# Differential attention with an expert gate: the copy of the gathered output rows is made by VectorE instead of ScalarE

## The reference, cut to what matters

```python
q, k, v = (einsum('bsd,od->bso', xn, w) for w in (wq, wk, wv))   # xn = layernorm(x), x is 4 x 1024 x 256
# 8 heads; q and k of each head are two maps (m = 0, 1) of 32 columns, v is 32 columns
attn = softmax(q @ k.T / sqrt(32) + causal, axis=-1)              # per head and map, 1024 x 1024
attn = attn[:, :nh] - attn[:, nh:] * lmbda                        # map 0 minus lambda times map 1
out = attn @ v                                                    # then an RMS norm in groups, and wo
x = x + (out_normed @ wo.T) * silu(ffn(xn))                       # ffn: 8 experts, 2 chosen for a row
```

## Time and profile before

| | |
|---|---|
| median of 3 runs | 1182.87 us (1180.96 to 1183.23) |
| the profiled execution, its own time | 1181.43 us |
| its span | 1179.8 us |
| attention (first scores to last `keep_half` copy) | about 184 to 821 us |
| busy over the span | PE 86%, DVE 81%, ACT 67%, POOL 17% |
| granted TensorE clock, mean | 0.948 of full speed |

### The profile page before, as it was taken

The page is one execution under the profiler, slowest core; times in us unless marked ns, Lnnn a source line. Parts: engine busy times, 40 slices in busy tenths (PEclk is TensorE's granted clock), DMA queues, the critical chain, the costliest instruction groups (busy, mean ns, idle before and its releaser), DMA issues. The chain is left out here.

```text
span 1179.8 us, 26028 instructions
## 1 busy us (share of the span) xinstructions
PE 1009.1 (86%) x6946; PEld 685.5 (58%) x6947; DVE 955.4 (81%) x1872; ACT 794.2 (67%) x1981; POOL 203.5 (17%) x296
## 2 busy tenths in 40 slices
PE   6888776699999999999999999997999999982565
PEld 4666554466666666666666666665555555551453
DVE  5576677699999999999999999995677777763887
ACT  3444345599999999999999999996333333334664
POOL 2000001021122211221112112220000000006772
PEclk9999986899999999999999999999999999995777
DMA  7988968874746565565657474740222222213553
GB/s 275 327 328 310 332 261 272 260 162 107 148 110 148 119 134 123 130 137 121 137 112 156 104 154 107 154 89 19 71 83 83 80 84 80 84 65 119 160 173 120
DMA packets 86587, 178.12 MB, mean 151 GB/s; under 512 B 11296, under 2 KB 46624, under 8 KB 84768
## 3 DMA queue, kind: packets, MB, share of 16 engines
q1 hardware_dynamic: 68512, 147.38, 46.2%
q0 software_dynamic: 7680, 20.98, 6.3%
q10 hardware_dynamic: 10368, 9.44, 2.3%
HBM read 108.56 MB, written 69.21 MB: 151 GB/s over the span
## 5 line engine op out<-in xcount | busy, mean ns | idle before, releaser
L1055 DVE TENSOR_REDUCE nmax<-bank 128x1 f32<-128x1024 f32 (+3 forms) x256 | 260.4, 1017 | 6.0 <-PE bank L857 4.2
L976 ACT ACTIVATE Pr_long<-bank,nmax 128x1024 f32<-128x1024 f32 (+3 forms) x256 | 250.5, 979 | 11.0 <-DVE nmax L1055 11.0
L1003 ACT COPY AT<-bank 128x512 f32<-128x512 f32 (+3 forms) x384 | 173.5, 488 | 18.2 <-PE bank L896 17.9
L896 PE MATMUL bank<-ident,Pr_long 128*128 128x128 f32 x832 | 142.2, 284 | 18.8 <-DVE Pr_long L1105 18.1
L990 ACT ACTIVATE Pr_short<-bank,nmax 128x128 f32<-128x128 f32 (+3 forms) x256 | 138.2, 540 | 22.1 <-DVE nmax L1073 21.5
L855 PE MATMUL bank<-Ks_first,Qs_first 128*128 128x512 f32 (+3 forms) x384 | 123.7, 412 | 27.2 <-ACTq L1029 10.5
L1247 PE MATMUL bank<-gu_sb,xsT 128*128 x288 | 139.7, 608 | 3.1 <-DVE hid L1364 0.6
L1105 DVE SCALAR_TENSOR_TENSOR Pr_long<-Pr_long,coef 128x1024 f32<-128x1024 f32 (+3 forms) x128 | 137.7, 1076 | 0.0
L936 PE MATMUL bank<-AT,Vj 128*32 128x128 f32 x2304 | 134.7, 282 | 0.2 <-ACT AT L1003 0.2
L855 PE MATMUL bank<-Ks_second,Qs_second 128*128 128x512 f32 (+3 forms) x384 | 119.7, 400 | 9.5 <-ACT Pr_long L976 4.9
L857 PE MATMUL bank<-maskb,identb 128*128 128x128 bf16 x512 | 117.8, 233 | 0.0
(11 more groups left out here) (149 smaller groups left out, 1683.4 us busy)
## 6 DMA issues: line engine op xcount, KB each, us to landing
q_parts<-PARTS SPq DMA_DIRECT2D x32, 512.0 KB, 3.5
k_parts<-PARTS SPq DMA_DIRECT2D x32, 512.0 KB, 3.7
Qs_first<-q_parts SPq DMA_DIRECT2D x64, 256.0 KB
Ks_first<-k_parts SPq DMA_DIRECT2D x64, 256.0 KB
Qs_second<-q_parts SPq DMA_DIRECT2D x64, 256.0 KB, 6.0
Ks_second<-k_parts SPq DMA_DIRECT2D x64, 256.0 KB, 6.8
xs_dram<-zeros SPq DMA_DIRECT2D x8, 1152.0 KB, 7.5
xs<-xs_dram SPq DMA_DIRECT2D x72, 128.0 KB, 2.0
```

The costliest lines, as they stand in the source:

```text
L896: last = nc.tensor.transpose(tb[fill % BANKS][:, i * P:(i + 1) * P], probs[:, 0, kb * P:(kb + 1) * P], ident[:])
L976: nc.scalar.activation(long_probs(p)[:, m, 0:N], long_slot[m][:, 0:N], ACT.Exp, bias=nmax[:, 4 * p + m:4 * p + m + 1], scale=1.0, accum_ou ...
L1003: nc.scalar.copy(AT[u % 4][:, 0:w], tb[unit_fill(p, k) % BANKS][:, 0:w]).then_inc(unit_out, 1)
L1055: nc.vector.tensor_reduce(nmax[:, 4 * p + m:4 * p + m + 1], long_slot[m][:, 0:N], AX.X, ALU.max, negate=True).then_inc(long_maxed, 1)
```

## The change

The copy `keep_half` moves from ScalarE's frame to VectorE's. It stands there between `max_short(p+3, 0)` and `max_long(p+3, 1)`, and waits for `gathered` of pair p as before. VectorE also gives the credit for `gather_out` at the start. The frames of both engines are written with other offsets now (ScalarE's by one pair less, VectorE's by two pairs more, with the number of frames ahead changed to suit), which by itself leaves the order of instructions on an engine as it was.

```diff
-                def keep_half(it, p):
-                    ...
-                    nc.scalar.wait_ge(gathered, credited(it, NP // 2, p // 2))
-                    ...
-                    nc.scalar.copy(to, tb[gather_fill(p) % BANKS][:, 0:4 * DH].rearrange(
-                        "p (a t d) -> p a t d", a=2, t=2)).then_inc(gather_out, 1)
                 @block.scalar
                 def _(act):
-                    act.sem_inc(gather_out, NP // 2)
                     def frame(it, p):
-                        exp_short(it, p + 3, 0)
-                        turn_out(it, p + 1, LONG1)
-                        keep_half(it, p)
-                        exp_long(it, p + 3, 1)
-                        out_tile(it, p + 1)
-                        exp_short(it, p + 3, 1)
-                        turn_out(it, p + 2, LONG0)
-                        turn_out(it, p + 2, SHORT)
-                        exp_long(it, p + 4, 0)
-                    run_pairs(act, 4, frame)
+                        exp_short(it, p + 2, 0)
+                        turn_out(it, p, LONG1)
+                        exp_long(it, p + 2, 1)
+                        out_tile(it, p)
+                        exp_short(it, p + 2, 1)
+                        turn_out(it, p + 1, LONG0)
+                        turn_out(it, p + 1, SHORT)
+                        exp_long(it, p + 3, 0)
+                    run_pairs(act, 3, frame)
+                def keep_half(it, p):
+                    ...
+                    nc.vector.wait_ge(gathered, credited(it, NP // 2, p // 2))
+                    ...
+                    nc.vector.tensor_copy(to, tb[gather_fill(p) % BANKS][:, 0:4 * DH].rearrange(
+                        "p (a t d) -> p a t d", a=2, t=2)).then_inc(gather_out, 1)
                 @block.vector
                 def _(dve):
+                    dve.sem_inc(gather_out, NP // 2)
                     def frame(it, p):
-                        ratio(it, p)
-                        max_short(it, p + 1, 0)
-                        max_long(it, p + 1, 1)
-                        combine_long(it, p)
-                        max_short(it, p + 1, 1)
-                        combine_short(it, p)
-                        max_long(it, p + 2, 0)
-                        inverse(it, p + 1)
-                    run_pairs(dve, 2, frame)
+                        ratio(it, p + 2)
+                        max_short(it, p + 3, 0)
+                        keep_half(it, p)
+                        max_long(it, p + 3, 1)
+                        combine_long(it, p + 2)
+                        max_short(it, p + 3, 1)
+                        combine_short(it, p + 2)
+                        max_long(it, p + 4, 0)
+                        inverse(it, p + 3)
+                    run_pairs(dve, 4, frame)
```

More of the change, by code:

```diff
@@ L1013, in out_tile @@
                     nc.scalar.copy(Ob[p // 2 % 2][:], ob[:]).then_inc(o_out, 1)
-                def keep_half(it, p):
-                    if absent(it, p) or p % 2 == 0:
-                        return
-                    it, p = place(it, p)
-                    nc.scalar.wait_ge(gathered, credited(it, NP // 2, p // 2))
-                    head, h = head_of(p), half_of(p)
-                    to = VO[:, bass.ds(it, 1), :, head * DH:(head + 1) * DH].rearrange(
-                        "p o (a t) d -> p (o a) t d", t=2)[:, h:4 - h:3 - 2 * h, :, :]
-                    nc.scalar.copy(to, tb[gather_fill(p) % BANKS][:, 0:4 * DH].rearrange(
-                        "p (a t d) -> p a t d", a=2, t=2)).then_inc(gather_out, 1)
                 @block.scalar
@@ L1119, in combine_short @@
                         in1=probs[:, 0, 0:N], op0=ALU.mult, op1=ALU.add).then_inc(short_combined, 1)
+                def keep_half(it, p):
+                    if absent(it, p) or p % 2 == 0:
+                        return
+                    it, p = place(it, p)
+                    nc.vector.wait_ge(gathered, credited(it, NP // 2, p // 2))
+                    head, h = head_of(p), half_of(p)
+                    to = VO[:, bass.ds(it, 1), :, head * DH:(head + 1) * DH].rearrange(
+                        "p o (a t) d -> p (o a) t d", t=2)[:, h:4 - h:3 - 2 * h, :, :]
+                    nc.vector.tensor_copy(to, tb[gather_fill(p) % BANKS][:, 0:4 * DH].rearrange(
+                        "p (a t d) -> p a t d", a=2, t=2)).then_inc(gather_out, 1)
                 @block.vector
                 def _(dve):
+                    dve.sem_inc(gather_out, NP // 2)
                     dve.sem_inc(long_maxed, 2 * NP)
```

## The result

The changed kernel takes 1234.68 us (median of 4 runs, 1233.73 to 1234.85) against 1181.91 (median of 4 runs, 1180.44 to 1183.23). The ratio is 1.0445, 95% interval 1.0427 to 1.0463: 52.8 us slower. The forecast was 1231, within 1211 to 1264. One execution of the kernel before, in a later set, took 1822.86 us in a slower state and is left out of the ratios.

The account below looks back on a forecast made before the run. No engine alone was taken to bound attention, but a ring of handovers among three. Waits and copies of 2.70 us less slack make 1.60 us a head; 30 x 1.60 + 0.4 = 48.4 us gives 1231, range 1211 to 1264.

Parts of the forecast that it names:

- the ring: In attention TensorE, VectorE and ScalarE pass work round, none alone the bound; what counts is who waits at each handover.
- delay by the wait, first gather: VectorE, p%4 = 1: the copy ahead of the long maximum waits for the gather; 1.04 us of wait.
- delay by the wait, second gather: VectorE, p%4 = 3: the copy ahead of the long maximum waits for the gather; 1.26 us of wait.
- given back by the two slacks: VectorE's two waits for scores in each head absorb 0.36 and 0.74 us of the delay.
- the handover: From the gather's end on TensorE to the copy's start on VectorE: 0.04 us.
- ScalarE's relief: ScalarE loses a copy taking 0.15 us of queue, twice a head; the gain was counted at nothing.
- First and last head: First head's delay ends in TensorE's 9.59 us wait for second-iteration keys; the last head costs 0.4 us.
- The copy's row: On VectorE, the 128-column copy from a bank lasts 0.285 us and takes 0.20 us of queue.
- Slack that gives nothing back: Rival, chance 0.14: both waits for scores stay in attention, costing 81 us, 1264.
- A shorter wait: Rival, chance 0.14: VectorE finds the gather nearer its end, 0.3 us less a wait, 18 us smaller: 1213.
- Only the copy's own time: Rival, chance 0.06: gathers are done when VectorE comes; 1183 if slack hides the copies, 1195 if not.
- Faster: Rival, chance 0.04: ScalarE is the bound, and 0.15 us is won at every gather: 9 us, 1174.

Follow-up runs that it names:

- The wait alone: Against the kernel before: ScalarE still copies; VectorE only waits for the gather at the changed kernel's copy place; 36.1 us over before, ratio 1.0305.
- the queue time alone: Against the kernel before: ScalarE still copies; VectorE runs an instruction of about the copy's length there, without waiting for another engine; 0.9 us over before.
- the copy one place later: Against the changed kernel: VectorE's copy stands behind the long maximum instead of ahead of it; 1.1 us over the kernel before, ratio 1.0009.
- one-gather kernels: Against the changed kernel: VectorE copies only a head's first, or only its second, gather, ScalarE the other; 27.4 and 21.6 us over the kernel before.
- the fixed place: Against the changed kernel: the copy goes to the same place of VO in every iteration, without loop-dependent address; 5.4 us less than the change, ratio 1.0399.
- no copy at all: Against the kernel before: the copy of gathered rows is left out on every engine, and TensorE doesn't wait for it; 0.2 us over before.
- Behind the short combination: Against the changed kernel: VectorE's copy stands three places later, behind the short combination; 4.4 us over the kernel before, ratio 1.0037.
- the earlier gather: Against the changed kernel: TensorE's gather goes ahead of the transposes of LONG1; 13.2 us less than the change, ratio 1.0333.

## Why the prediction was right

**The mechanism** was the one that was forecast: a copy set ahead of the long maximum makes VectorE wait for the gather, and what stands behind it goes round the ring. The wait alone, the queue time alone and the copy one place later show it separately.

**The terms**, for one head; measured from the rows above:

| term | forecast | measured |
|---|---|---|
| delay by the wait, first gather | 1.04 | 1.15 |
| delay by the wait, second gather | 1.26 | 1.37 |
| two copies | 0.40 | 0.41 |
| given back by the two slacks | -1.10 | -1.15 (the balance) |
| head | 1.60 | 1.78 |

A delay is taken against the moment at which the long maximum would have started without the copy. At the first gather that moment is set by its scores: in the kernel before it starts 0.05 and 0.04 us behind the end of their mask in the two sorts of heads (506.76 + 0.23 = 506.99 to 507.04; 526.04 + 0.23 = 526.27 to 526.31).

```profile
506.76 0.23 PE L857 MATMUL bank<-maskb,identb 128*128 128x128 bf16 x1
...
526.04 0.23 PE L857 MATMUL bank<-maskb,identb 128*128 128x128 bf16 x1
...
526.31 1.23 DVE L1055 TENSOR_REDUCE nmax<-bank 128x1 f32<-128x1024 f32 x1
```

In the changed kernel the mask ends at 509.54 + 0.23 = 509.77, so the moment is 509.81 and the delay 510.96 - 509.81:

```profile
509.54 0.23 PE L857 MATMUL bank<-maskb,identb 128*128 128x128 bf16 x1
```

At the second gather the long maximum starts 0.48 behind the short one (509.54 - 509.06 in the first of the one-gather kernels), which makes 521.33 - 519.96. The copies are 511.17 - 510.96 and 521.53 - 521.33.

**What was mis-sized** is the handover. I took 0.04 us from the last iteration, which is unrolled; in the loop it is 0.15, because the copy's address is made behind the wait. Each of the two delays is 0.11 longer than forecast, and this is all of it: TensorE's part, from the mask's end to the gather's end, is 508.04 - 506.99 = 1.05 us before and 510.81 - 509.77 = 1.04 in the changed kernel. Over 28 heads in the loop 0.22 us is 6 us; the fixed place measured 5.4. The copies and the slack, which gave back 0.05 more than forecast, leave 0.18 a head. One thing stays unexplained: in the changed kernel the heads in the loop alternate at 20.98 and 21.08 us (first short maxima at 509.28, 530.26 and 551.34), where before they lasted 19.19 and 19.23 (506.59, 525.78 and 545.01); the terms are of the shorter sort.

**The slack** was right in kind: each wait for scores took the delay ahead of it, and both went to zero. **ScalarE's relief**, counted at nothing, was nothing (no copy at all: 0.2 us). **First and last head** were right: the delay of the first vanished in the wait for keys; in the last head the second copy stands 5.8 us behind the first (867.43 to 873.26), where it was 5.4 (815.15 to 820.55), the 0.4 of the forecast. 30 heads of 1.78 us are 53.4 us, against 52.8 measured for the medians. **The copy's row** is 0.29 us and takes 0.20 to 0.21 of the queue; forecast 0.285 and 0.20. The Trainium skill, page "VectorE: DVE Perf Modes", section on the TRN2 errata, gives 0.258 us for it by the estimate in the prediction; the trace has 0.03 more.

**The rivals.** Slack that gives nothing back would have been 30 x 2.93 = 88 us with the measured delays; it was 53. A shorter wait: it was longer. Only the copy's own time: 0.9 us when tried alone. Faster: excluded by the kernel without a copy.

**Where I was wrong** is in expectations, not in the forecast. Behind the short combination I counted neither the prediction's own premise, that work is hidden only ahead of a wait, nor the turn that waits for the bank, and the runs don't say which of the two cost the 4.4 us; for the earlier gather I took 20 us where 13 came; and each of the one-gather kernels came out 3 us under its range.

## What to carry to other kernels

When an instruction moves to another engine, ask first what it waits for and what will stand behind it there: here 0.2 us of work cost 0.9 us a gather ahead of an instruction that could have run, and nothing one place further down. Idle time in a queue hides work that stands ahead of the wait (that it hides nothing behind it is likely here, but not shown), and each wait has to be checked by itself, since a delay that gets past one shifts the next wait and its cause together. Equal busy shares of 93% on three engines don't say that any of them is the bound; taking the copy from ScalarE altogether changed nothing.

## What the runs showed that was not expected

A copy in a loop whose destination depends on the loop's register starts 0.15 us after the gather that it waits for, against 0.04 us with a fixed address, as in the unrolled iterations; 56 such waits in the loop cost 5.4 us of 1182 by the fixed place, which no longer has the register operation of 0.06 us. I had expected the address to be ready before the wait ends.
